# VectorE and ScalarE work put in another order in the attention tiles of a two-layer convolution and attention kernel

## The reference, cut to what matters

```
x = x + L0(_gn(x))          # group norm; four depthwise 3x3 convolutions (value, query, key, offset);
                            # sampling points = tanh(offset + ref); bilinear samples of value;
                            # attn = q.k^T * SCALE; out = attn . v_sampled; projection w_out
x = x + L1(_gn(x))          # per pixel (token) of 384 channels:
  xn  = layer_norm(xs) * ln_g + ln_b
  mid = silu(xn @ fc1_w + fc1_b) @ fc2_w + fc2_b          # 384 -> 1536 -> 384
  q, k, v = xs @ qkv_w ; q, k normalised per head (8 heads of 48)
  o = 0.5 * v + 1/pi * q (k^T v) ; o normalised per head ; o = o + mid
  out = o @ proj_w + proj_b
```

## Time and profile before

| | |
|---|---|
| median of 3 runs | 2845.35 us |
| profiled execution: its own time | 2844.07 us |
| its span | 2842.3 us |
| PE (matmul) busy | 2735.0 us, 96% |
| DVE busy | 1993.1 us, 70% |
| ACT busy | 1184.6 us, 42% |
| POOL busy | 692.6 us, 24% |

### The profile page before, as it was taken

How to read it: one execution, slowest core, us unless ns; L and a number is a source line. 1 busy time by engine, 2 the same in 40 slices (tenths; PEclk the granted TensorE clock), 3 DMA queues, 4 the chain that set the end, 5 groups by cost and what they waited for, 6 DMA issues and landing times.

```text
span 2842.3 us, 40695 instructions
## 1 busy us (share of the span) xinstructions
PE 2735.0 (96%) x14670; PEld 2489.6 (88%) x14670; DVE 1993.1 (70%) x2519; ACT 1184.6 (42%) x2043; POOL 692.6 (24%) x211
## 2 busy tenths in 40 slices
PE   6998699999999999999999999999999999999999
PEld 4555699899998899899998899999999899999998
DVE  5968794988887693988887693888887633443433
ACT  3341366444432265444443266344443254333332
POOL 0011052322224053322224043322224033221220
PEclk8998799999999999999999999999999999999999
DMA  5237642333346733333337743234436832111210
GB/s 220 58 112 244 216 134 83 100 100 101 102 122 202 266 115 103 97 102 101 100 101 211 262 134 93 67 111 112 121 100 187 286 97 73 43 43 45 54 43 30
DMA packets 206758, 347.55 MB, mean 122 GB/s; under 512 B 24160, under 2 KB 190176, under 8 KB 203744
## 3 DMA queue, kind: packets, MB, share of 16 engines
q1 hardware_dynamic: 180528, 311.59, 33.9%
q10 hardware_dynamic: 21552, 14.05, 3.8%
q0 software_dynamic: 4480, 19.27, 2.4%
HBM read 241.31 MB, written 103.56 MB: 121 GB/s over the span
## 4 chain that ended last, share of the span: by engine, by line
PE 66%; issue 17%; DMA 6%; DVE 4%; POOL 4%; ACT 2%; SPq 0%; ACTq 0%; DVEq 0%; POOLq 0%
PE bank L756 14%; PE bank L758 13%; PE bank L757 13%; PE bank L802 4%; PE bank L961 3%; PE bank L963 3%; PE bank L962 3%; PE bank L983 3%; PE bank L1146 3%; PE bank L1132 2%; DMA X<-x_scr 2%; POOL rq L674 1%; POOL ro L678 1%; PE bank L1099 1%; DMA X0Q<-in_x 1%
## 5 line engine op out<-in xcount | busy, mean ns | idle before, releaser
L1726 ACT ACTIVATE S<-bank,b1p 128x448 f32<-128x448 f32 x336 | 212.8, 633 | 845.1 <-PE bank L758 818.3
L2363 DVE SCALAR_TENSOR_TENSOR AC<-XV,wfold,AC 128x1568 f32<-128x1568 f32 x288 | 530.4, 1847 | 2.7
L756 PE MATMUL bank<-SH,W2H 128*128 128x448 f32 x1008 | 389.6, 387 | 3.1 <-DVE SL L2332 3.1
L756 PE MATMUL bank<-XRH,W1H 128*128 128x448 f32 x1008 | 377.6, 375 | 0.0
L758 PE MATMUL bank<-SH,W2L 128*128 128x448 f32 x1008 | 375.9, 373 | 0.0
L757 PE MATMUL bank<-SL,W2H 128*128 128x448 f32 x1008 | 374.2, 371 | 0.0
L757 PE MATMUL bank<-XRL,W1H 128*128 128x448 f32 x1008 | 374.2, 371 | 0.0
L758 PE MATMUL bank<-XRH,W1L 128*128 128x448 f32 x1008 | 373.0, 370 | 0.0
L674 POOL TENSOR_TENSOR rq<-qn,nhalf 112x32 f32<-112x32 f32 x28 | 181.9, 6495 | 407.0 <-DVE qn L2302 407.0
L666 POOL TENSOR_TENSOR rk<-kn,nhalf 112x24 f32<-112x24 f32 (+1 forms) x56 | 200.5, 3591 | 298.1 <-DVE kn L2140 298.1
L2332 DVE TENSOR_TENSOR SL<-S,SH 128x448 fp32r<-128x448 f32 x336 | 207.7, 619 | 76.2 <-ACT SH L1729 76.1
(11 more groups left out here) (228 smaller groups left out, 5234.8 us busy)
## 6 DMA issues: line engine op xcount, KB each, us to landing
X<-x_scr SPq DMA_DIRECT2D x52, 672.0 KB, 5.1
XV<-in_xp SPq DMA_DIRECT2D x36, 870.0 KB, 7.7
XC<-in_xp SPq DMA_DIRECT2D x14, 1682.0 KB, 10.4
CQ<-q_scr SPq DMA_DIRECT2D x28, 672.0 KB
CX<-in_x SPq DMA_DIRECT2D x28, 672.0 KB, 5.0
x_scr<-CX SPq DMA_DIRECT2D x28, 672.0 KB, 5.8
V<-v_scr SPq DMA_DIRECT2D x28, 672.0 KB, 7.0
Y<-x_scr SPq DMA_DIRECT2D x28, 672.0 KB
```

The costliest lines, as they stand in the source:

```text
L756: mm(o, wh, xh, start=first, stop=False)
L1726: fn(S[:, j % 2, :], bank[j % 2][:, 0:T], ACT.Silu, bias=b1p[:, j:j + 1]).then_inc(s["s_s"], 1)
L2363: stt(o, XV[h][:, ky:ky + HR, kx:kx + W], wfold[:, kind, k, 3 * ky + kx:3 * ky + kx + 1], o, ALU.mult, ALU.add).then_inc(s["va"], 1)
```

## The change: what it does

Six edits, none of which adds or removes an instruction:

1. DVE, tile 0 of images 0 to 2: `sampling_points` stands at the end of tile 0 instead of in tile 1 behind `strip_stats`; on ACT, `tanh` goes in tile 0 behind silu 8 instead of behind the tile.
2. DVE, every tile: `split_s(n, 0)` stands ahead of `conv(t, 0)`.
3. DVE, tiles 1 to 3 of images 0 to 2: `split_x(t + 1)` stands behind `split_s(n, 2)`.
4. ACT, tiles 1 to 3 of images 0 to 2: `norm_in` stands behind the copy of group 3 of the unit instead of behind silu 1.
5. ACT, tile 0: `attended_h` stands ahead of silu 7.
6. DVE, tile 0: `attended_l` stands ahead of `split_s(n, 7)`, and `conv(t, 6)` behind it.

```
 # ScalarE, tile(n, t)
                     silu(n, 1)
-                    if not last:
+                    if not last and not before:
                         norm_in(b * KVX + STRIPS + t + 1)
                     silu(n, 2)
...
                     if before:
                         unit_out(t - 1, 1, 3)
+                        norm_in(b * KVX + STRIPS + t + 1)
...
+                    if first:
+                        attended_h(n, first)
                     silu(n, 7)
-                    if not last:
+                    if not first and not last:
                         attended_h(n, first)
                     for j in range(8, JC - 1):
                         silu(n, j)
+                        if nxt and first and j == 8:
+                            tanh(b + 1)
 # VectorE, tile(t, n)
+                    split_s(n, 0)
                     conv(t, 0)
-                    split_s(n, 0)
...
-                    if nxt and t == 1:
-                        sampling_points(b + 1)
...
                     if last:
                         o_final(n)
-                    else:
+                    elif not before:
                         split_x(t + 1)
                     split_s(n, 2)
+                    if before:
+                        split_x(t + 1)
...
-                    conv(t, 6)
+                    if first:
+                        attended_l(n)
+                    else:
+                        conv(t, 6)
                     split_s(n, 7)
                     if first:
-                        attended_l(n)
+                        conv(t, 6)
...
                     conv(t, 10)
+                    if nxt and first:
+                        sampling_points(b + 1)
```

More of the change, by code:

```diff
@@ L1841, in image @@
                     tile(n0 + t, t)
-                    if nxt and t == 0:
-                        tanh(b + 1)
                 if nxt:
@@ L2367, in tile @@
                     first, last = t == 0, t == STRIPS - 1
+                    before = nxt and 1 <= t <= KC
                     if not first:
                         output(n - 1)
+                    split_s(n, 0)
                     conv(t, 0)
-                    split_s(n, 0)
                     if nxt and t >= 1:
```

## The result

The changed kernel takes 2883.2 us (median of 4 runs, 2880.67 to 2889.34) against 2844.95 us of the kernel before: ratio 1.0147, 95% interval 1.0113 to 1.0181. It is 1.5% slower. The profiled execution took 2889.34 us, 45.3 us more than that of before and 6 us more than its own median, so sums over the two traces come out a little larger than the ratio.

What follows compares the result with a forecast made beforehand. PE sets a tile's length; only 10.0 us of its waits, 0.35% of 2844 us, could be won directly. Terms 9.6 + 12.0 + 4 + 3 = +28.6 us gave 2873 us, 1.0% slower; range 2847 to 2889.

Steps and rivals of the forecast that it cites:

- rival C: Each of nine new waits of 2.7 us and more lowers PE's clock: 15 us more, 2888 us; chance 0.20.
- `turn_x`, tiles 2 and 3: norm_in behind the copy of group 3 makes turn_x 1.60 us later in six places: +9.6 us; other bound -3.8.
- `turn_x`, tiles 1 (from the tile's start): Y finished 2.97 us later delays store, copy and norm_in; turn_x 4.6 and 3.4 us later, 12.0 us for three images.
- behind `turn_x`, tiles 1 to 3: Late split_x delays token statistics, rr and query_norms: 0.3 us per tile, +3 us for nine, bounds 0 and 11.
- tiles 4 and 5: Split 0 ahead of the tap idles DVE 1.4 us; PE waits 0.7 us in six tiles: +4 us, bounds 0 and 8.4.
- that the store lands behind Y: Tiles 2 and 3: group 0's store, issued earlier, still lands behind 672 KB Y in one queue; copy still starts at 628.76.
- split 7 is therefore possible at about 512.4 as before: Tile 0, image 0: split 7 keeps its time; two taps and X behind it end at 518.2 against 517.44, 0.7 us later.
- about 1.5: Expected sign: PE waits for SL in step 0 of tile 1 about 1.5 us.
- nine times 2.5 to 5 us: Expected sign: a new row of PE waits, bank L1099 behind ACT X, nine times 2.5 to 5 us.
- A: The waits go and nothing takes their place: -10.0 us, 2834 us; chance 0.07.
- B: The store is not held up by Y: +3 to +5 us, 2848 us; chance 0.11.
- the formula beside it: Skill's rule: a DMA takes about 2.0 us plus bytes over 436 GB/s, so a 224 KB store 2.5 us.

Runs made afterwards that it cites:

- experiment 7: The changed kernel with SP issuing the store of a unit's group 0 ahead of the load of Y in tiles 1 to 3: 1.0046 of the kernel before.
- experiments 1: Kernel before with only norm_in moved behind the copy of group 3, split_x left ahead of split 2: 1.0159.
- experiment 2: Kernel before with norm_in behind the copy of group 3 and split_x behind split 2 in tiles 1 to 3: 1.0073.
- experiment 5: Kernel before with only MH and ML put ahead of silu 7 and split 7 in tile 0: 1.0003.
- experiment 3: Kernel before with only tanh and sampling_points moved to the end of tile 0, ahead of Y: 1.0022.
- experiment 4: Kernel before with only split 0 put ahead of the tap, in every tile: 1.0012.
- experiment 8: Kernel before with norm_in behind the copies of groups 0 to 2, ahead of silu 3, and split_x behind split 2: 1.0001.
- experiments 6: The changed kernel with norm_in and split_x back where they stood before, the other four edits kept: 1.0055 of the kernel before.

## Why the prediction was right, and where its sizes were off

The forecast was 2873 us, +28.6; measured +38 us between the medians and +42 by the ratio, inside the range. The direction and the main mechanism were right. That the time fell inside the range is in part owed to rival C, for whose sake the range was drawn up to 2889: the forecast's own sum has no term for the clock, and by the ratio (2887 us) and in the profiled execution (2889.34) the time came out at rival C's 2888. The forecast's own range, 2860 to 2883, just reaches the median of 2883.2. In the two traces, forecast and measured:

| part | forecast, us | measured, us |
|---|---|---|
| `turn_x`, tiles 2 and 3 | +9.6 | +9.6 |
| `turn_x`, tiles 1 (from the tile's start) | +12.0 | +16.9 |
| behind `turn_x`, tiles 1 to 3 | +3 | +10.8 |
| tiles 4 and 5 | +4 | +7.7 |
| all the rest | 0 | +0.3 |

By its steps:

**Edits 3 and 4 in tiles 2 and 3: right, in mechanism and size.** Forecast 6 x 1.60 = 9.6 us. Measured from each tile's first matmul, `turn_x` comes 1.41, 2.01, 1.84, 1.32, 1.81 and 1.18 us later than before: 9.6 us. The step it rests on, that the store lands behind Y, is shown by experiment 7, and by the copy's 5.06 us behind Y's issue. That the sum agrees to a tenth is luck: the single places lie between 1.18 and 2.01. What the prediction left out is that this size needs edit 3: it never priced edit 3, and without it the loss is 24 us larger (experiments 1 and 2).

**Tile 1: right in kind, too small.** Forecast 12.0 us; from the tile's first matmul `turn_x` came 4.9, 5.5 and 6.5 us later, 16.9 us. The forecast counted from the start of tile 0, with PE's gain there included; so counted the three are 5.5, 5.9 and 3.0 us, 14.4 in all. The third is small only because tile 0 of image 2 took 86.3 us before, at a granted clock of 0.90, and 82.7 us after at 0.96. The mis-sized step is the place of qn in tile 0: "split 7 is therefore possible at about 512.4 as before", qn at 518.2, +0.7 us. Where the earlier trace rows stood, the trace has:

```profile
511.31 1.42 ACT L1744 ACTIVATE MH<-bank 128x448 fp32r<-128x448 f32 x3 [3.19 <-PE bank L1201]
511.89 1.69 DVE L2340 TENSOR_TENSOR ML<-bank,MH 128x448 fp32r<-128x448 f32 x3 [1.43 <-ACT MH L1744]
513.90 0.62 DVE L2335 TENSOR_TENSOR SL<-S,SH 128x448 fp32r<-128x448 f32 x1 [0.32 <-ACT SH L1729]
...
519.56 0.18 DVE L2305 COPY qn<-bank 112x32 f32<-112x32 f32 x1
```

MH waits for PE until 511.31, silu 7 stands behind it, and the two taps that had filled this time on DVE now stand behind split 7: DVE idles 1.43 + 0.32 us, split 7 comes at 513.90 and qn 2.1 us later than before, not 0.7. DVE has no pause in which to regain it (its wait for rq hangs on qn), so Y begins 5.66 us into tile 1 (551.68 - 546.02) instead of 1.66, 4.0 us later, not 2.97. The load of Y, the store, the copy and `turn_x` follow in the forecast's order, with the copy at 564.16 instead of 563.23. In image 2, rq alone takes 2.3 us longer than elsewhere as well (last section). PE's wait for the first SL of tile 1 is 2.6 to 4.3 us, not "about 1.5", for the same reason; experiment 5 shows it (3.5, 2.0 and 2.3 us) from edits 5 and 6 alone, experiment 3 (2.8 to 2.9 us) from edit 1 alone. And since PE has stood there already, its waits at `turn_x` are shorter than the forecast's "nine times 2.5 to 5 us": 1.7 to 3.6, five of them under 2.5. So PE's gain in tile 0 is paid back in tile 1, by the delay of DVE.

**Tiles 4 and 5: right in kind.** Forecast six waits of 0.7 us in step 1, +4 us. The trace after has six of 0.41 to 0.51 us (2.9 us: the 12.5 us for SL less 9.6 us in the tiles 1), and the six tiles grew by 7.7 us. The rest is clock, for which the forecast had no term: six stretches at half against three before, 5.1 us. All nine stand behind `query_norms` and none behind the new waits, so that edit 2 caused them is not shown; in the other traces that were read in the same way these tiles lose 3.4 to 10.2 us. By itself (experiment 4) this edit cost 0.0012, not told apart from nothing.

**Behind turn_x: the wrong cause.** Here the forecast failed. It priced 3 us of delay passed on by `split_x`; tiles 1 to 3 lost 37.3 us, `turn_x` 26.5 of them, and the other 10.8 go with 11.9 us of lost clock, which was rival C. C's price for one stretch at half (1.6 us) was right, 1.7 measured. Its condition, that each new wait brings one (at its end or right behind it), is right for six of the nine waits at `turn_x` (one of them, 3.58 us, has two in a row), for none of the other three (2.39, 2.25 and 1.68 us), and also for the 4.33 us wait for SL. In experiment 2 it is three of nine: waits of 2.46, 2.03 and 2.02 us have one behind them, those of 2.57, 2.27 and 2.19 us and the three shorter ones have none. So a longer wait makes it no certainty, and what decides stays open. The stretches at half that have no wait before them follow `query_norms` (last section): eight before, seven after.

**The rivals.** A (the waits go, nothing in their place) could not have come true from ACT's order alone: experiment 8 shows that `turn_x` waits for the copy of group 3 too. B (the store isn't held up by Y) is refuted by experiment 7; the formula beside it, from the Trainium skill (page DMA: Bandwidth & Descriptors, section Anatomy of one DMA), has terms for a fixed cost and for bytes and none for what lies ahead in the queue. The least of 2.5 us fits it, while stores behind Y took up to 7.2 us.

## What to carry to other kernels

Before putting work behind an instruction, ask what that instruction waits for when nobody is in its way: here it was a 224 KB store queued behind a 672 KB load, and the remedy stood in SP's order, not in ACT's. A small store whose buffer is wanted soon goes ahead of a large load that isn't wanted soon. When a producer is moved later, its consumers on other engines must be moved behind what they would block: that one edit was worth more (24 us) than all the waits the change went for (10 us). And a sum of waits is not yet a time: of the 45 us between the two traces some 17 were clock.

## What the runs showed of the chip

- Short stands of PE often cost more than their length. Stretches behind the waits at `turn_x` in tiles 1, 2 and 3 of image 0 of the kernel after (granted clock, third number from the end; 0.50 is 1.2 GHz):

```profile
566.20:569.60 3.40, 2.85 (x12) 2.76 (x13) 2.83 (x3) 3.39 (x6) 0.00 (x0) 0.50 0.12 31
638.00:641.50 3.50, 3.37 (x14) 3.22 (x15) 3.35 (x3) 3.47 (x7) 0.00 (x0) 0.53 0.01 3
709.00:712.50 3.50, 3.02 (x12) 2.92 (x13) 3.00 (x3) 3.47 (x7) 0.00 (x0) 0.58 0.10 26
```

  Behind the 2.39 us wait of tile 2 in image 1 of the same kernel there is none, behind the 2.46 us wait at the same place in experiment 2 there is one:

```profile
1303.50:1308.00 4.50, 4.01 (x24) 3.80 (x25) 3.99 (x3) 3.91 (x7) 0.00 (x0) 1.00 0.07 20
```

```profile
1284.10:1288.10 4.00, 3.58 (x14) 3.43 (x15) 3.57 (x3) 3.83 (x7) 0.00 (x0) 0.57 0.07 18
```

- The clock also falls where PE has no wait. All eight stretches at half in tiles 1 to 3 of the kernel before, 40 to 41 us into their tiles, follow the 24 small matmuls (128x8) of `query_norms`, which the profile counts as busy. In tile 1 of image 0 these run from 583.75 to 586.18, and then:

```profile
586.00:589.50 3.50, 3.50 (x12) 3.12 (x12) 3.50 (x5) 0.00 (x0) 0.94 (x1) 0.52 0.77 247
```

  Not every tile has one (the second of image 0 has none), and no run shows why.
- One POOL instruction sometimes took a third longer. In tile 0 of image 2 of the kernel after, rq took 9.26 us; its median over 28 places is 6.97 us, and before the longest was 6.97, and the wait for the first SL of the tile behind it is the longest of its kind (4.33 us against 2.64 and 2.66):

```profile
1843.24 9.26 POOL L674 TENSOR_TENSOR rq<-qn,nhalf 112x32 f32<-112x32 f32 x1 [11.16 <-DVE qn L2305]
```

  The same 9.26 us, once among 28, stand in the traces of experiments 6 and 7 (tile 0 of image 0), and in none of the other eleven. No run shows why.
